# Flamingo gated stack on one core: group 1's first attention in layer 1's banks and buffers, filler turnings placed anew

## The reference

```python
x = x + jnp.tanh(g_xattn[0]) * _L0_xattn_ref(_layernorm(x), ctx_1024, ctx_1024, ...)
x = x + jnp.tanh(g_ffn[0]) * _L0_ffn_ref(_layernorm(x), w_gate, w_up, w_down)
x = x + jnp.tanh(g_xattn[1]) * _L1_xattn_ref(_layernorm(x), ctx_1024, ctx_1024, mask, ...)
x = x + jnp.tanh(g_ffn[1]) * _L1_ffn_ref(_layernorm(x), ...)
# layer 0's attention, 16 heads of 8:
qn = _l2_rownorm(q); kn = _l2_rownorm(k)
scores = jnp.einsum('bhqd,bhkd->bhqk', qn, kn)
attn = scores * scores
out = jnp.einsum('bhqk,bhkd->bqhd', attn, v) ... @ Wo_w.T + Wo_b
# layer 0's feed-forward, all operands rounded to FP4 by blocks of 16:
h = silu(fp4_linear(x, w_gate)) * fp4_linear(x, w_up); return fp4_linear(h, w_down)
```

## Time and profile before

| | us |
|---|---|
| median of 3 runs | 758.95 |
| lowest and highest | 755.32 and 759.46 |
| profiled execution | 757.0 |
| its span, first to last instruction | 754.5 |
| TensorE busy | 704.5 |
| VectorE busy | 536.6 |
| ScalarE busy | 412.2 |
| GpSimd busy | 215.9 |

### The profile page before, as it was taken

How to read it: one execution, slowest core, us unless ns; L and a number is a source line. 1 busy time by engine, 2 the same in 40 slices (tenths; PEclk the granted TensorE clock), 3 DMA queues, 4 the chain that set the end, 5 groups by cost and what they waited for, 6 DMA issues and landing times.

```text
span 754.5 us, 19091 instructions
## 1 busy us (share of the span) xinstructions
PE 704.5 (93%) x8046; PEld 506.3 (67%) x8046; DVE 536.6 (71%) x1150; ACT 412.2 (55%) x680; POOL 215.9 (29%) x543
## 2 busy tenths in 40 slices
...
DMA packets 23971, 12.65 MB, mean 17 GB/s; under 512 B 6408, under 2 KB 23376, under 8 KB 23888
## 3 DMA queue, kind: packets, MB, share of 16 engines
...
## 4 chain that ended last, share of the span: by engine, by line
PE 78%; DVE 9%; ACT 6%; POOL 4%; issue 2%; DMA 1%; POOLq 0%; DVEq 0%
PE A L877 18%; PE B L877 17%; PE Y L877 16%; PE H L877 15%; PE B L1123 3%; PE H L886 3%; PE A L881 2%; PE B L881 2%; ACT A L395 2%; ACT hid L395 1%; ACT xn L400 1%; DMA cin<-in_ctx_dram 1%; PE A L1019 1%; POOL hs L316 1%; POOL hs L306 1%
## 5 line engine op out<-in xcount | busy, mean ns | idle before, releaser
L877 PE MATMUL H<-xmT,w_s 128*128 128x512 f32 x256 | 137.4, 618 | 7.8 <-ACT hid L395 7.8
L395 ACT ACTIVATE hid<-H,b_s 128x512 f32<-128x512 f32 x128 | 87.7, 685 | 95.0 <-PE H L877 94.5
L877 PEld LDWEIGHTS Y<-w_s,hid 128*128 128x128 f32 x1024 | 121.3, 192 | 19.9 <-issue 17.2
L306 POOL TENSOR_TENSOR hs<-stats 128x4 f32<-128x4 f32 x48 | 16.9, 353 | 411.0 <-DVE stats L605 410.9
L877 PE MATMUL Y<-w_s,hid 128*128 128x128 f32 x1024 | 126.4, 277 | 2.2 <-DVE acc L854 1.4
L854 DVE SCALAR_TENSOR_TENSOR acc<-Y,wgt,acc 128x128 f32<-128x128 f32 x256 | 71.8, 343 | 49.0 <-PE Y L877 48.4
L886 PE MATMUL H<-ident 128*128 128x128 f32 x510 | 64.9, 280 | 1.7 <-POOL ident L294 1.7
L886 PEld LDWEIGHTS H<-ident 128*128 128x128 f32 x510 | 58.9, 144 | 4.9 <-issue 2.2
L877 PEld LDWEIGHTS H<-xmT,w_s 128*128 128x128 f32 x256 | 39.0, 189 | 31.6 <-ACT hid L395 18.6
L795 DVE TENSOR_REDUCE mx<-B 128x16 f32<-128x1024 f32 x32 | 39.1, 1223 | 18.7 <-PE B L877 18.4
L316 POOL TENSOR_TENSOR hs<-hs,mhalf 128x4 f32<-128x4 f32 x48 | 50.7, 1055 | 3.8
...
## 6 DMA issues: line engine op xcount, KB each, us to landing
...
```

The lines of the kernel that those rows point to most:

```text
L306: pl.tensor_tensor(w[:, 0], st[:, :, 1], st[:, :, 4], ALU.subtract)
L395: return act.activation(dst, source, f, **kw)
L877: return pe.matmul(o, l, r, start=start, stop=stop)
```

## The change

Layer 0's attention of group 1, and of no other group, gets other banks and buffers. `OTHER = (1,)` names the group; `of(g, name)` gives set 0 or set 1, and `bank_of(stage, g)` turns A2 into B2 and A1 into B1 for all `a_` stages of group 1. Set 1 is made of buffers of layer 1 that are empty at that time: xmT for qk, P4 for the squares, qT4 and hT4 for the turned k and q, oT4 for oX, pT1 for the norm's small buffers, and `pool`, a new name for the memory of hid and acc together, for vz0. GpSimd sets pool to zero at the start, one memset more, and VectorE waits for it at group 1's a_k. `before(g)` gives the group that used the same vz0 last.

```diff
-        qk2 = A0[:, 1].rearrange("p (w t d) -> p w t d", w=2, t=T)
+        def squares(a0):
+            return a0[:, 1].rearrange("p (w t d) -> p w t d", w=2, t=T)
...
-        hid = sb("hid", [2, FCH, N]); acc = sb("acc", [2, T, P])
+        pool = sb("pool", [2 * FCH * N + 2 * N])
+        hid = pool[:, 0:2 * FCH * N].rearrange("p (a c n) -> p a c n", a=2, c=FCH)
+        acc = pool[:, 2 * FCH * N:2 * FCH * N + 2 * N].rearrange("p (a t d) -> p a t d", a=2, t=T)
...
+        OTHER = (1,)
+        def before(g):
+            same = [q for q in range(g) if (q in OTHER) == (g in OTHER)]
+            return same[-1] if same else -1
+        set0 = dict(A2=A2, A1=A1, qk=qk, A0=A0, kT0=kT0, hT0=hT0, vz0=vz0, oX=oX, ss=ss, ssh=ssh, rs=rs, rs2=rs2)
+        set1 = dict(A2=B2, A1=B1, qk=xmT[:].rearrange("p a (t d) -> p a t d", t=T), A0=P4, kT0=qT4, hT0=hT4,
+                    vz0=pool[:].rearrange("p (x n d) -> p x n d", n=Q4, d=48),
...
+        def of(g, name):
+            return (set1 if g in OTHER else set0)[name]
+        def bank_of(stage, g):
+            b = BANK[stage]
+            return {"A2": "B2", "A1": "B1"}[b] if stage[0] == "a" and g in OTHER else b
...
-            after(pe, free[BANK[stage]], FREED[stage, k, g] - READERS.get(stage, 1))
+            after(pe, free[bank_of(stage, g)], FREED[stage, k, g] - READERS.get(stage, 1))
...
+                pl.memset(pool[:], 0.0).then_inc(setup, 1)
...
-                    copy(kT0[:], A20).then_inc(free["A2"], 1)
+                    copy(of(g, "kT0")[:], of(g, "A2")[:, 0:512]).then_inc(free[bank_of("a_kt", g)], 1)
...
-                    filled(ve, "a_av", g - 1)
+                    filled(ve, "a_av", before(g))
+                    if g == OTHER[0]:
+                        ve.wait_ge(setup, 9)
...
-        w.20:0 a_ctx:0 w.5:0 a_w:0 w.17:0 a_ctx:1 a_kv:0 w.15:0 a_wo:0 w.5:0 a_n1t:0 w.5:0 a_q:0 w.87:0 f_w:0 f_wd:0
+        w.20:0 a_ctx:0 w.5:0 a_w:0 w.16:0 a_ctx:1 a_kv:0 a_wo:0 w.27:0 a_n1t:0 w.23:0 a_q:0 w.29:0 f_wd:0 w.11:0
```

More of the change, by code:

```diff
@@ new lines @@
+        a_s0.1:1 a_sh.1:1 w.8:0 a_s0.2:1 a_sh.2:1 a_av.1:1 a_s0.3:1 a_av.2:1 a_sh.3:1 w.8:0 a_av.3:1 f_qht:0 f_qhu:0
+        a_o0:1 f_dn:0 c_kv:0 a_ctx:2 w.7:0 a_kv:2 a_q:2 w.24:0 c_n3t:0 w.7:0 c_q1:0 w.15:0 c_s:0 w.9:0 f_qxt:1 w.5:0
+        f_gu.0:1 w.13:0 c_pt:0 a_n1t:3 f_gu.1:1 c_av:0 a_qt:2 f_gu.2:1 c_kv:1 a_ctx:3 a_kt:2 w.6:0 a_s0.0:2 a_sh.0:2
+        s_n4t:0 f_gu.3:1 s_k4:0 s_v4:0 a_av.0:2 a_s0.1:2 a_sh.1:2 s_q4:0 a_s0.2:2 s_s.0:0 a_sh.2:2 s_sh.0:0 a_av.1:2
+        a_s0.3:2 a_av.2:2 a_sh.3:2 s_s.1:0 s_sh.1:0 a_av.3:2 w.5:0 a_o0:2 s_t.0:0 w.8:0 s_s.2:0 s_sh.2:0 a_kv:3
```

380 lines of the change are left out of this document (190 added, 190 removed).

## The result

The changed kernel takes **747.76 us** (median of 6 runs, 743.96 to 750.19), the kernel before 757.75 (median of 6): ratio 0.9862, interval 0.9838 to 0.9887, some 10 us less. The direction was right, the size about half.

The account below looks back on a forecast made before the run. Bound: group 0's dependent chain in the first 110 us, then VectorE, and from 190 to 720 us TensorE's fixed work. 757.0 - 7.2 (gains) + 2.3 (one clock fall) + 1.0 (profile to median) = 753.1 us, range 747 to 759.

Parts of the forecast that it names:

- Front: Start of group 0 up to TensorE's turning of q and k: at 35.0 instead of 36.14, gain 1.1 us.
- Scores: Group 0's scores up to xr: pauses filled, a_o0 at 50.8, xr at 52.9; gain 2.9 us, nearly all clock.
- From xr to the product: Group 0 from VectorE's xr to f_qxt: a_k:1 now done before xr; gain 0.5 us.
- f_gu and f_qh: Four f_gu steps, a_kt:1 no longer in A2: gain 1.4 us; f_qh no longer behind a square on ScalarE: 0.6.
- Hand-over: To layer 1, from f_qht to a_k:2 on VectorE: 11.3 us instead of 12.0, gain 0.7.
- Sum 7.2: All gains from the front through the hand-over to layer 1, in us; VectorE's full queue fixes the rest.
- Fillers and falls: Idle of about 2.7 us ahead of a_n1t:2 may lower the clock: bounds 0 and 2.3 us, 2.3 taken off once.
- B: Rival: full clock up to f_dn, 750.8 us; down to 747 without low clock after the 3.41 wait (3.0); chance 0.25.
- The later queues are re-sorted by a place or two; their real work is the same.: Queue orders of the later part, costed at nothing.
- Rival D: Gain ends in a wait, possibly the idle before c_n3t:1, so the end does not move: 758.0 us; chance 0.09.

Follow-up runs that it names:

- e14: The changed kernel with front fillers moved: 20 instead of 27 ahead of a_n1t:0, 7 instead of 23 ahead of a_q:0, 46 instead of 29 behind it; 747.61 us.
- e3: The changed kernel with twelve entries of VectorE's order, around xh of group 1 and its moments, put back as in the kernel before; 750.47 us.
- e7: The changed kernel with its banks up to c_n3t:0 (about 106 us), the orders of the kernel before on all five queues from there; 751.40 us.
- e10: The changed kernel with 90 instead of 65 fillers behind a_o0:0, ahead of a_n1t:2; 747.13 us.
- e12: The changed kernel with two entries of GpSimd's order exchanged: c_n3:1 (moments of xh) ahead of a_xr:3; 747.40 us.
- e13: The changed kernel with f_dn:1 alone two norm steps earlier in VectorE's order; 751.03 us.
- e5: The kernel before with 30 filler turnings put into the idle 3.41 us ahead of c_n3t:1, nothing else; 754.85 us.

## Why the prediction was wrong in size

- **Front, forecast 1.1.** 1.32: qk turned at 34.82, forecast 35.0, and VectorE's a_q came at 25.62, forecast 25.7. Right. The context came 0.31 later in this execution; counted from its turning the gain is 1.63 (22.70 to 21.07). It could have been 1.5 more (e14, 19.60), since 23 fillers held a_q:0 back behind an input that was there; I costed them as they stood and didn't ask whether they were longer than the wait they fill.
- **Scores, forecast 2.9, all clock.** 1.34 in this execution, because the clock fell at 49 instead of 46: a_q:1 took 2.08 and a_o0:0 came at 51.97, not 50.8. In the profiles of e3, e7, e10, e12 and e13, whose code is the same up to there, the scores stayed at full clock and the gain was 2.88. Sized right for the executions without a fall.
- **From xr to the product, forecast 0.5.** 1.25. Too low. The first FP4 step on xr starts 6.66 behind it in both kernels; all of the 1.25 lies between there and the last one (6.71 and 5.46), where steps of group 1's norm stand between those of FP4. Which of them gives it no run shows.
- **f_gu and f_qh, forecast 1.4 and 0.6.** 2.01. Right: the four steps are 3.1 apart and ScalarE took FP4's magnitudes at 85.63, 0.03 behind their input.
- **Hand-over, forecast 0.7.** From FP4 of h to a_k:2 on VectorE it is 13.04 (103.40 - 90.36) where it was 13.74. Right.
- **Sum 7.2 up to the full queue of VectorE.** 7.05 at c_av:0, with part of the scores' gain missing and 0.75 and 0.4 more than forecast behind xr and in the hand-over to c_av:0. That the sum comes so near is in part luck. e7 shows that it is passed on.
- **Fillers and falls, forecast 2.3 once.** The gap of 2.7 was there, and a fall behind it in three of six profiles, at 1.1 to 2.7 us each. The size was right; what I left out is that the fall behind the wait of 3.41 could go. B names it (3.0, which is what e5 measured) but took it for the odd case.
- **"The later queues are re-sorted by a place or two; their real work is the same."** This is the step that failed: a term put at nothing. The work is the same, and a few places on VectorE are worth 5.84 us in the profile: 3.6 of engines holding each other up and 3.0 of clock behind the shorter wait, less 0.77 of c_av:0 to xh:1. Rival D had looked at just this place and had the sign wrong. It counted the two norm steps that went ahead of xh as delay, and not that they had stood between xh and its moments, beside what GpSimd starts when xh is read. The two rows of the kernel before that show it, 1.40 and 2.59, were in its trace and not in the prediction. In the medians the step is smaller: the change without the twelve entries (e3, 750.47) or with f_dn:1 moved back alone (e13, 751.03) is 2.7 and 3.3 above the changed kernel, out of the 5.3 by which the forecast was too high.
- **The other 2 to 2.6 us.** The forecast took 2.9 off for the clock in the scores and put 2.3 back for a fall, so it left nearly as much low clock as there was. In the executions of e3 and e13 it is 11.2 and 12.4 us on average, where before has 19. That this gives the rest is argued from these averages; no run isolates it.

Put together: 757.0 - 7.05 - 5.84 + 0.39 is 744.5, beside the profiled execution's 744.3. The median lies 3.4 above it, since most of the six have more low clock (9 us in the profiled one, 12 on average).
